# Attention: the product with V in four column groups of 32, row sums by ones from exponentials added in pairs

## The reference

```python
scores = jnp.einsum('bhqd,bhkd->bhqk', q, k) * scale
scores = jnp.where(causal, scores, jnp.finfo(scores.dtype).min)
probs = jax.nn.softmax(scores, axis=-1)
attn = jnp.einsum('bhqk,bhkd->bhqd', probs, v)
```

## Time and profile before

| | |
|---|---|
| Median of 3 runs | 1939.92 us (1938.9 to 1941.08) |
| The profiled execution | 1941.45 us |
| Its span, first to last instruction | 1939.3 us |
| Busy: PE, DVE, ACT, POOL | 1864.7, 1118.7, 696.0, 375.8 us |
| Attention stage | about 220 to 825 us |
| TensorE's granted clock, mean | 0.983 |

### The profile page before, as it was taken

The page is one execution under the profiler, slowest core; times in us unless marked ns, Lnnn a source line. Parts: engine busy times, 40 slices in busy tenths (PEclk is TensorE's granted clock), DMA queues, the critical chain, the costliest instruction groups (busy, mean ns, idle before and its releaser), DMA issues.

```text
span 1939.3 us, 23895 instructions
## 1 busy us (share of the span) xinstructions
PE 1864.7 (96%) x8448; PEld 1324.0 (68%) x8448; DVE 1118.7 (58%) x1690; ACT 696.0 (36%) x1112; POOL 375.8 (19%) x355
## 2 busy tenths in 40 slices
PE   5995899999999999899999999999999999999997
PEld 4784455545454545347888888888888888888886
DVE  4510665656565656545767566756665666567643
ACT  2311455655565555402323222222322232223221
POOL 3303000111110110102222222222222222222221
PEclk9998799999999999999999999999999999999999
DMA  6565404404414310052110111011101110110002
GB/s 213 167 224 149 97 10 93 84 20 87 86 26 83 80 37 4 12 206 65 33 33 0 32 32 32 0 32 32 32 0 32 32 32 0 32 32 0 0 1 87
DMA packets 88856, 109.30 MB, mean 56 GB/s; under 512 B 44248, under 2 KB 60632, under 8 KB 85008
## 3 DMA queue, kind: packets, MB, share of 16 engines
q1 hardware_dynamic: 88784, 108.39, 20.8%
HBM read 75.09 MB, written 29.59 MB: 54 GB/s over the span
## 4 chain that ended last, share of the span: by engine, by line
PE 56%; DVE 0%; ACT 0%; POOLq 0%; issue 0%; POOL 0%
PE p_gate L50 6%; PE p_gate L49 6%; PE p_gate L48 6%; PE p_out L48 6%; PE p_out L50 6%; PE p_out L49 6%; PE p_up L50 6%; PE p_up L49 6%; PE p_up L48 6%; PE p_out L1140 1%; PE p_gate L1140 1%; PE p_up L1140 1%; DVE acc L1075 0%; POOLq L831 0%; DVE inter L1055 0%
## 5 line engine op out<-in xcount | busy, mean ns | idle before, releaser
L590 ACT ACTIVATE e_sb<-p_st 128x512 f32<-128x512 f32 (+3 forms) x640 | 295.5, 549 | 261.6 <-PE p_st L741 139.5
L639 DVE TENSOR_REDUCE max_part<-p_s 128x1 f32<-128x512 f32 x384 | 240.6, 683 | 74.5 <-PE p_s L716 74.0
L764 PE MATMUL p_o<-e_sb,v_stack 128*33 128x512 f32 (+5 forms) x1280 | 251.0, 535 | 0.0
L716 PE MATMUL p_s<-k_stack,q_stack 96*128 96x512 f32 (+3 forms) x640 | 225.1, 406 | 22.4 <-DMA k_stack<-qk_scratch 19.7
L999 POOL TENSOR_SCALAR poly<-poly 128x1024 f32<-128x1024 f32 x64 | 71.2, 1112 | 876.4 <-ACT poly L966 876.4
L741 PE MATMUL p_st<-q_stack,k_stack 128*128 128x512 f32 (+3 forms) x640 | 226.2, 401 | 10.9 <-ACT e_sb L590 7.4
L1055 DVE SCALAR_TENSOR_TENSOR inter<-inter,gate 128x1024 f32<-128x1024 f32 x64 | 78.4, 1225 | 255.2 <-ACT inter L971 254.5
L635 DVE CUSTOM_DVE_ANT_0 masked_scores<-p_s,score_mask 128x128 f32<-128x128 f32 (+3 forms) x256 | 119.1, 487 | 165.6 <-PE p_s L716 163.4
L48 PE MATMUL p_out<-i_hi,w_hi 128*128 128x512 f32 x512 | 200.0, 391 | 3.1 <-DVE acc L1075 3.1
L50 PE MATMUL p_out<-i_hi,w_lo 128*128 128x512 f32 x512 | 199.8, 390 | 0.0
L49 PE MATMUL p_out<-i_lo,w_hi 128*128 128x512 f32 x512 | 199.7, 390 | 0.0
(11 more groups left out here) (103 smaller groups left out, 2613.1 us busy)
## 6 DMA issues: line engine op xcount, KB each, us to landing
q_stack<-qk_scratch SPq DMA_DIRECT2D x48, 256.0 KB, 7.3
k_stack<-qk_scratch SPq DMA_DIRECT2D x48, 256.0 KB, 8.5
qk_scratch<-out_hi SPq DMA_DIRECT2D x32, 256.0 KB, 2.6
qk_scratch<-out_lo SPq DMA_DIRECT2D x32, 256.0 KB, 3.2
scales<-in_gate_up_s SPq DMA_DIRECT2D x128, 64.0 KB, 2.3
x_sb<-in_x SPq DMA_DIRECT2D x4, 1024.0 KB, 12.8
xn_lo_scratch<-xn_lo_made SPq DMA_DIRECT2D x1, 4096.0 KB, 12.7
v_scratch<-out_v SPq DMA_DIRECT2D x16, 256.0 KB, 2.0
```

The costliest lines, as they stand in the source:

```text
L590: nc.scalar.activation(e_sb[:, x % E_BUFS, :, 0:w], p_st[:, x % ST_BUFS, :, 0:w], ACT.Exp, scale=SCALE).then_inc(exp_done, 1)
L639: nc.vector.reduce_max(part, p_s[:, slot[n] % S_BUFS, 0:w], AX.X).then_inc(maxed, 1)
L716: nc.tensor.matmul(p_s[:, slot[n] % S_BUFS, 0:w], q_stack[p % PB][a][0:ROWS, i * P:(i + 1) * P], k_stack[p % PB][a][0:ROWS, b * W:b * W + ...
L764: last = nc.tensor.matmul(p_o[a * VW:a * VW + width, q0:], v_stack[p % PB][:, kt, a, 0:width], e_sb[:, x % E_BUFS, a if PH == 2 else 0, 0: ...
```

## The change

1. p_o becomes two halves: 128 rows by 256 columns for the product and as many for the sums. product_v makes up to four matmuls a step, (head a, half h of the queries), each of 32 columns of V by 256 queries, into rows (2a + h) x 32. The columns of ones in v_stack are gone.
2. For each pair of steps of a group and each head (SUMS = 4 a group) the two exponential tiles are added elementwise into one of 6 tiles e_sum: by DVE for the last of the four in full groups (after the group's second unit), by POOL for the others. On the diagonal the wider tile's first 128 columns have no partner.
3. New on PE: row_sums(k) after the products of group k. It waits for the group's sums and multiplies them by ones into the second half of p_o: 8 matmuls of 256 columns, on the diagonal 10 of 128 or 256.
4. An exponential tile is free again when its product and its sum are made, on the diagonal for the even steps also row_sums; there are 15 tiles in place of 16.
5. copy_out waits for row_sums. A chunk is stored by 8 DMAs (4 before). V is loaded by one DMA a pair (2 before). masked_scores, which is only written, is BF16. divide takes one reciprocal of 256 columns over 128 rows and four products of 32 x 256.

```diff
-    E_BUFS = 16
+    E_BUFS = 15
+    def summed(k, m):
+        g = GS * k + 2 * (m // 2)
+        q0, q1 = STEPS[g % NS][2], STEPS[(g + 1) % NS][2]
+        return g * PIECES + m % 2, (g + 1) * PIECES + m % 2, q1 - q0, W - q1
+
+    def made_by_vector(k, m):
+        return m == SUMS - 1 and not DIAG[GS * k % NS]
...
         @block.gpsimd
+            def sum_steps(k, part, before):
+                for m in part:
+                    if k < 0 or k >= NG or made_by_vector(k, m):
+                        continue
+                    n = SUMS * k + m
+                    x, y, skip, w = summed(k, m)
+                    pool.wait_ge(exp_done, y + 1)
...
+                    if n >= SUM_BUFS:
+                        pool.wait_ge(rows_done, (n - SUM_BUFS) // SUMS + 1)
+                    nc.gpsimd.tensor_tensor(e_sum[:, n % SUM_BUFS, 0:w], e_sb[:, x % E_BUFS, skip:skip + w],
+                                            e_sb[:, y % E_BUFS, 0:w], ALU.add).then_inc(pool_summed, 1)
...
             for k in range(-1, NG):
+                sum_steps(k, (2, 3), products)
                 for p, r in BATCHES[k]:
                     split(p, r, products)
                     splits += 1
+                sum_steps(k + 1, (0, 1), products)
                 p, s = divmod(GS * k, NS)
                 if p > 0 and s in (24, 28, 32, 36):
-                    normalise(p - 1, products % TC, splits)
+                    normalise(p - 1, products % TC, splits, pool_sums[min((k + 1, 1), (NG - 1, SUMS - 1))])
...
         @block.scalar
                 if x >= E_BUFS:
-                    act.wait_ge(pv_done, piece(x - E_BUFS)[0] + 1)
+                    old = piece(x - E_BUFS)[0]
+                    j, i = divmod(old, GS)
+                    act.wait_ge(pv_done, old + 1)
+                    if DIAG[old % NS] and i % 2 == 0:
+                        act.wait_ge(rows_done, j + 1)
+                    m = 2 * (i // 2) + (x - E_BUFS) % PIECES
+                    if made_by_vector(j, m):
+                        act.wait_ge(vector_summed, vector_sums[j, m])
+                    else:
+                        act.wait_ge(pool_summed, pool_sums[j, m])
...
         @block.vector
+                units = units_of(k)
+                if not units:
+                    sum_steps(k)
+                for n in units:
                     unit_max(n)
+                    if n == units[0] + 1:
+                        sum_steps(k)
...
         @block.tensor
             def product_v(g):
...
-                width = ONE if p < PAIRS - 1 else VW
-                for a in range(2):
-                    x = g * PIECES + (a if PH == 1 else 0)
-                    last = nc.tensor.matmul(p_o[a * VW:a * VW + width, q0:], v_stack[p % PB][:, kt, a, 0:width],
-                                            e_sb[:, x % E_BUFS, a if PH == 2 else 0, 0:W - q0], start=kt == 0,
-                                            stop=s in CHUNK_END)
+                for h in range(2):
+                    first, end = max(q0, h * HALF), (h + 1) * HALF
+                    for a in range(2):
+                        if first < end:
+                            last = nc.tensor.matmul(p_o[(2 * a + h) * D:(2 * a + h + 1) * D, 0, first - h * HALF:],
+                                                    v_stack[p % PB][:, kt, a, :],
+                                                    e_sb[:, (g * PIECES + a) % E_BUFS, first - q0:end - q0],
+                                                    start=kt == 0, stop=False)
                 last.then_inc(pv_done, 1)
+
+            def row_sums(k):
+                p, s = divmod(GS * k, NS)
+                for m in range(SUMS):
+                    if made_by_vector(k, m):
+                        pe.wait_ge(vector_summed, vector_sums[k, m])
+                    else:
+                        pe.wait_ge(pool_summed, pool_sums[k, m])
+                def add(a, h, first, end, what, stop):
+                    return nc.tensor.matmul(p_o[(2 * a + h) * D:(2 * a + h + 1) * D, 1, first:end], ones[:, :], what,
+                                            start=False, stop=stop)
+                if DIAG[s]:
...
+                else:
+                    for j in range(2):
+                        for h in range(2):
+                            for a in range(2):
+                                n = SUMS * k + 2 * j + a
+                                last = add(a, h, 0, HALF, e_sum[:, n % SUM_BUFS, h * HALF:(h + 1) * HALF], False)
+                last.then_inc(rows_done, 1)
...
                 for g in range(GS * k, GS * k + GS):
                     product_v(g)
+                row_sums(k)
                 some_units(7, 8)
```

More of the change, by code:

```diff
@@ L383, in attention @@
         k_stack = [[sb(f"k_stack{i}{a}", [P, S], F32R) for a in range(2)] for i in range(PB)]
[L384 to L387, removed]
+        v_stack = [sb(f"v_stack{i}", [P, TT, 2, D], F32) for i in range(PB)]
+        e_sb = sb("e_sb", [P, E_BUFS, W], F32)
+        e_sum = sb("e_sum", [P, SUM_BUFS, W], F32)
+        ones = sb("ones", [P, D], F32)
+        o_sb = sb("o_sb", [P, 2, 2, HALF], F32)
+        recip = sb("recip", [P, HALF], F32)
         rsum_rows = sb("rsum_rows", [P, S], F32)
@@ L513, in _ @@
             nc.gpsimd.memset(max_cols[:, :, :, :], 0.0).then_inc(consts, 1)
+            nc.gpsimd.memset(ones[:, :], 1.0).then_inc(consts, 1)
             pool.wait_ge(consts, NC)
@@ L669, in divide_last @@
[L669 to L678, removed]
-                                            recip[rows + D:rows + VW, :], ALU.mult).then_inc(divided, 1)
+                if qc == TC - 1:
+                    dve.wait_ge(rows_done, NG)
+                    o = p_o[:, :, :]
+                else:
+                    dve.wait_ge(o_copied, c + 1)
+                    o = o_sb[:, c % 2, :, :]
@@ new lines, in divide @@
+                if qc:
+                    dve.wait_ge(divided, 4 * qc)
+                nc.vector.reciprocal(recip[:, :], o[:, 1, :]).then_inc(inverted, 1)
+                dve.wait_ge(inverted, qc + 1)
+                for a in range(2):
+                    for h in range(2):
+                        rows = slice((2 * a + h) * D, (2 * a + h + 1) * D)
+                        nc.vector.tensor_tensor(attn_rows(p, a, qc)[:, h * HALF:(h + 1) * HALF], o[rows, 0, :],
+                                                recip[rows, :], ALU.mult).then_inc(divided, 1)
@@ new lines, in sum_steps @@
+            def sum_steps(k):
+                for m in range(SUMS):
+                    if made_by_vector(k, m):
+                        n = SUMS * k + m
+                        x, y, skip, w = summed(k, m)
+                        dve.wait_ge(exp_done, y + 1)
+                        if n >= SUM_BUFS:
+                            dve.wait_ge(rows_done, (n - SUM_BUFS) // SUMS + 1)
+                        nc.vector.tensor_tensor(e_sum[:, n % SUM_BUFS, 0:w], e_sb[:, x % E_BUFS, skip:skip + w],
+                                                e_sb[:, y % E_BUFS, 0:w], ALU.add).then_inc(vector_summed, 1)
@@ L740, in scores_t @@
                     pe.wait_ge(exp_done, x - ST_BUFS + 1)
[L741 removed]
+                last = nc.tensor.matmul(p_st[:, x % ST_BUFS, 0:W - q0], k_stack[p % PB][a][:, kt * P:(kt + 1) * P],
                                         q_stack[p % PB][a][:, qc * W + q0:(qc + 1) * W], start=True,
@@ L749, in mask_t @@
                 if piece(x)[0] < NSTEP:
-                    nc.tensor.matmul(p_st[:, x % ST_BUFS, 0, 0:P], ident[:, :], mask_k[:, :], start=False,
+                    nc.tensor.matmul(p_st[:, x % ST_BUFS, 0:P], ident[:, :], mask_k[:, :], start=False,
                                      stop=True).then_inc(st_ready, 1)
```

98 lines of the change are left out of this document (57 added, 41 removed).

## The result

The changed kernel takes 1963.33 us (median of 4 runs, 1961.79 to 1966.28), the kernel before 1940.5 beside it: a ratio of 1.0119, 95% interval [1.0101, 1.0136]. It is slower by 22.8 us. The profiled execution has a span of 1961.5 us, 22.2 more than before's.

What follows compares the result with a forecast made beforehand. Attention was taken as bound by TensorE's own queue. Six pairs at +3.3 us gave +20, first pair 0, last pair and end -3: +17 on 1941.45 made 1958.5, median 1957, put at 1955; range 1912 to 1980.

Steps and rivals of the forecast that it cites:

- the waits eating the gain and more: Main case: TensorE's new waits in attention outweigh the cheaper product; 1944 to 1980 us, chance 0.50.
- The product and the sums: TensorE's product with V plus row sums: full group 2.71 us against 3.56, diagonal 2.70 against 2.28; 27 us less in all.
- four column groups don't run side by side: Rival on TensorE's product: only two column groups overlap, 124 us more, 2065 us; chance 0.10 for fewer than four.
- the estimate from the Trainium skill's factor for three tiles: TensorE's product: four column tiles at 3.15 times one tile's rate, adding some 0.66 us per full group, 30 us per run.
- the middle between halves that overlap and halves that don't: Diagonal groups' row sums on TensorE: 1.07 us, between 0.86 and 1.29, making the group 0.42 us dearer.
- first rival: Sums in time: row_sums never waits for POOL; about 1917 us, 1908 to 1935 if partly so; chance 0.27.
- POOL's order: POOL's queue: sums of 1.34 us stand behind the split, so TensorE's row_sums waits 0.5 to 1.2 us in k = 3, 4, 6, 9.
- the price that decides: POOL's time per sum deciding whether the three sums behind a split reach TensorE in time: 1.03 us.
- The exclusion: DVE and POOL wait for each other reading two SBUF operands: DVE's sum delays POOL 0.7 us or is delayed up to 1.27.
- The fifteenth tile: With 15 tiles, k = 9's eighth exponential waits for row sums, maxima copies behind it on ACT: k = 0 starts 0.85 us later.
- The last pair: Last head pair, no units or splits after k = 2: -1.4 us, plus -1.6 from the final division.

Runs made afterwards that it cites:

- experiment 3: All sums on POOL against the changed kernel: in its order 1959.51 us; with sums 0 and 1 of the next group ahead of the split, 1910.57 us.
- Experiment 2: Changed kernel with only POOL's queue reordered, sums 0 and 1 of the next group ahead of this group's split: 1941.91 us, ratio 1.0003.
- experiment 5: Copies of the maxima moved ahead of diagonal groups' eighth exponential: 1956.22 us on the changed kernel, 1903.66 with POOL's sums ahead of its split and all sums on POOL.
- bufs16: Changed kernel with 16 exponential tiles in place of 15 and one masked_scores buffer in place of two: 1950.76 us, ratio 1.0056.
- order_all_pool_maxima: Changed kernel with POOL's sums ahead of its split, all sums on POOL, and maxima copies ahead of diagonal groups' eighth exponential: 1903.66 us, ratio 0.9809.

## Why the prediction was right

The forecast was 1955, with the waits eating the gain and more as the likeliest case, and that case came. The sum before rounding was +17; the clock apart, the trace has +17.3. That it is so close is in part luck: single terms are off by up to 0.8 us a pair and cancel. Rounding down from 1957 to 1955, because I thought the doubtful terms high, was wrong: k = 0, 3, 6 and 9 all came out above them. By k, for a pair in which the clock doesn't fall:

| k | predicted | measured | |
|---|---|---|---|
| 0 | +1.15 | +1.33 | copies of the maxima late |
| 1 | -0.55 | -0.56 | |
| 2, 5 | +0.4 each | +0.25 each | diagonal product too dear |
| 3 | +0.2 | +0.36 | POOL's sums late |
| 4 | +0.1 | -0.11 | POOL's sums late, behind DVE's |
| 6 | +0.65 | +0.83 | DVE's sum late, not POOL's |
| 7 | -0.2 | +0.50 | DVE's sum late |
| 8 | +0.15 | -0.66 | DVE's sum undelayed, costs 0.3 |
| 9 | +1.0 | +1.18 | POOL's sums late |
| sum | +3.3 | +3.4 | |

**The product and the sums.** 2.71 predicted, 2.72 to 2.73 measured. Of the rival "four column groups don't run side by side" nothing is left, and the estimate from the Trainium skill's factor for three tiles ("TensorE: Matmul & The Clock Gate", Part 3), which I weighed there, falls with it: four groups run at twice the rate of two here, 0.215 us for a round of 256 columns. (That estimate was also added up low: at 3.15 a full group would get 0.70 us, not 0.66, and the 30 us leave out the diagonal groups.) On the diagonal I took the middle between halves that overlap and halves that don't. The timeline of k = 5 (start, us, what, count) shows that they overlap:

```profile
503.12 1.29 PE L821 MATMUL p_o<-e_sb,v_stack 128*32 128x256 f32 x18
504.03 0.41 PE L837 MATMUL p_o<-e_sb,ones 128*32 128x128 f32 x4
...
504.45 0.39 PE L821 MATMUL p_o<-e_sb,v_stack 128*32 128x128 f32 x4
```

The first half's row sums (L837) start at 504.03, while the second half's products still run to 504.84, although they stand behind them in the queue. The price is +0.25, near the lower bound of 0.2, where I used 0.42: a term that was mis-sized, by 0.17 us four times a pair. It is 5.4 us in eight pairs, and most of why a kernel with all sums in time takes 1910.6 (experiment 3) and not the 1917 of the first rival.

**POOL's order.** Right in mechanism and in size. Five sums in a row take 1.33 us each; I had 1.34. In k = 3 POOL's sums begin behind the split and TensorE's row sums go at 489.94 (timeline; idle before in brackets):

```profile
485.93 3.76 POOL L568 TENSOR_TENSOR e_sum<-e_sb 128x512 f32<-128x512 f32 x3
...
487.02 1.93 PE L821 MATMUL p_o<-e_sb,v_stack 128*32 128x256 f32 x32
...
489.94 1.07 PE L837 MATMUL p_o<-e_sum,ones 128*32 128x256 f32 x16 [0.98 <-POOL e_sum L568]
```

The product would let the row sums in at 487.02 + 1.75 = 488.77, and the third sum, at 485.93 + 3.76 = 489.69, is what is awaited. In k = 9 my terms add up to 6.87 us, not 7.05, and 128 columns take 0.45 us, where I had 0.35; the group came out at +1.18 against +1.0. I had set the price that decides at 1.03 us a sum. Experiment 2 adds what I didn't weigh: with a price of 1.33, another order does as well.

**The exclusion.** The mechanism was right, its place in part wrong. k = 6 of pair 3:

```profile
508.43 6.66 POOL L568 TENSOR_TENSOR e_sum<-e_sb 128x512 f32<-128x512 f32 x5
508.51 1.74 DVE L729 TENSOR_TENSOR e_sum<-e_sb 128x512 f32<-128x512 f32 x1
...
510.91 0.50 PE L772 MATMUL p_s<-k_stack,q_stack 96*128 96x512 f32 x1 [1.39 <-DVE max_part L687]
```

POOL's first sum begins 0.08 us ahead of DVE's, and DVE's takes 1.74 us, 1.05 more than its 0.69. The maximum behind it is late, the seventh unit waits 1.39, and the scores phase grows by 1.67 us; by the time the product is done, POOL's sums are there. I had the group at 8.5 us because of POOL; it takes 8.67 because of DVE: with POOL's order mended it still takes that (+0.82 in experiment 2), without DVE's sum it is at -0.14. In k = 7 DVE's sum starts beside POOL's after the normalisation and takes 1.61; I had counted half of what that costs (0.65 for what became 1.33), and in k = 8, where POOL rests, I had counted 1.0, of which 0.3 came. The two errors cancel to 0.1, which is luck. The Trainium skill, "SBUF — State Buffer", section "Who interferes with whom", has the rule: a VectorE instruction with two SBUF inputs contends with a GpSimd instruction that reads SBUF, and whichever starts first holds the pair to its end. The trace agrees, on both sides: in k = 6 POOL's sum goes first and DVE's waits; in k = 4 of this pair DVE's goes first, at 493.69, POOL's follows 0.03 us later and takes 1.79. The durations (ns, min/median/max):

```profile
L729 DVE TENSOR_TENSOR e_sum<-e_sb x48: 680/687/1740, 228.1 to 837.0; 128x512 f32<-128x512 f32 x48
...
L568 POOL TENSOR_TENSOR e_sum<-e_sb x272: 449/1266/1788, 211.1 to 842.2; 128x512 f32<-128x512 f32 x72, 128x384 f32<-128x384 f32 x32, 128x128 f32<-128x128 f32 x32
```

**The fifteenth tile.** Right: after the row sums of k = 9 ACT makes the eighth exponential, then the two copies, and TensorE waits at the start of k = 0.

```profile
538.90 0.28 ACT L639 ACTIVATE e_sb<-p_st 128x128 f32<-128x128 f32 x1 [4.18 <-PE p_o L837]
539.20 1.07 ACT L619 ACTIVATE q_stack<-p_s 32x512 fp32r<-32x512 f32 x2
...
539.85 1.21 PE L797 MATMUL p_st<-q_stack,k_stack 128*128 128x512 f32 x3 [0.87 <-ACT q_stack L619]
```

It costs 1.08 us in place of the 0.85 that I took; experiment 5 removes just that.

**The last pair.** -3.0 predicted, -4.6 measured. k = 0 to 7 go as reckoned (-1.1 against -0.95). The rest, -3.5 against -2.05, is the clock that didn't fall in the last product (-1.7). The division gave 1.2 us of the 1.6 that I took: the reciprocal fell from 3.36 to 1.76 us, but four products of 32x256 take 1.78 where two of 32x512 took 1.41, and I had 1.45.

```profile
844.02 1.76 DVE L713 RECIPROCAL recip<-p_o 128x256 f32<-128x256 f32 x1 [6.34 <-PE p_o L837]
845.82 1.78 DVE L718 TENSOR_TENSOR acc<-p_o,recip 32x256 f32<-32x256 f32 x4
```

**What I didn't have.** The clock. I read 1.00 in all ten groups of the earlier trace rows and took it as given, while my own sum put stands of about a microsecond into a queue that had none. It was worth 4.4 us net here; with it the sum for the profiled execution would have been 1941.45 + 17 + 4.4 = 1962.9, and it took 1963.27.

**What stays open.** Why one buffer of masked scores or the sixteenth tile takes 1.0 us from k = 6 to 8 in bufs16: it isn't the pairs' earlier start, and I didn't part the two. And why the clock falls after the same stand of 1.39 us in some pairs and not in others: only that it differs from pair to pair and from kernel to kernel is shown.

## What to carry to other kernels

Work that is moved to an idle engine costs by its place in that engine's queue, not by its sum: put what the bound engine needs soon ahead of anything that waits, and don't let VectorE and GpSimd both read two SBUF operands at once. A new wait of a microsecond on TensorE is to be priced with a chance of its clock falling behind it, here 1.2 to 1.7 us each time it did. When a buffer is taken away, look at everything that stands behind the instruction that now waits for it; here a change of order on ScalarE gave back the 7 us that the missing buffer cost, without the price of another buffer.

## What the runs showed of the hardware

- Four column groups of 32 run fully side by side in fp32: a round of four passes of 256 columns every 0.215 us, loads included, in 0.43 at the lower clock.
- Matmuls for one column group pass those of another that stand ahead of them in the program: the first half's row sums start 0.8 us before the second half's products end.
- The clock fell to 1.2 GHz for some 3.4 us right after a stand of 1.4 us in a stretch where TensorE was busy otherwise, in three of six identical groups. It also fell in k = 0 after two stands of 0.9 us, and in the kernel before at 812 us, after several of 0.2 to 0.4 (so too at 751 us in the last pair of order_all_pool_maxima). In the runs with POOL's new order and all sums on POOL, where no wait in the inner pairs is longer than 0.9 us, it never fell in those pairs.
- A DVE sum of 0.69 us takes up to 1.74 beside POOL's, a POOL sum of 1.27 up to 1.79 beside DVE's; the one that waits is the one that starts second, if only by 0.08 us.
